# The mixture of 32 experts by sorted token rows instead of every expert on every token

## The reference, cut to what matters

```python
x2 = _layernorm(src, ln2_g, ln2_b)
sel = jax.nn.sigmoid(x2 @ sel_w)
scores, idx = jax.lax.top_k(sel, K)
gate = (jax.nn.one_hot(idx, E, dtype=sel.dtype) * scores[..., None]).sum(-2)
h = jax.nn.relu(jnp.einsum('bsd,edh->bseh', x2, keys))
moe_out = jnp.einsum('bseh,ehd,bse->bsd', h, values, gate)
return src + moe_out
```

## Time and profile before

| what | value |
|---|---|
| median of 3 runs | 2990.05 us (2985.18 to 2991.54) |
| the profiled execution: time, span | 2985.78 us, 2983.8 us |
| PE busy | 2806.0 us, 94% |
| POOL busy | 2039.4 us, 68% |
| DVE, ACT busy | 1951.9 us (65%), 1852.1 us (62%) |
| mean granted PE clock | 0.974 of full speed |

### The profile page before, as it was taken

One profiled execution on the slowest core, in us unless ns is written; L12 is line 12 of the kernel. 1 busy time (PEld: TensorE's weight loads), 2 busy tenths in 40 slices (PEclk: granted clock), 3 DMA queues, 4 the chain that ended last, 5 costly groups with the idle time before them and its releaser, 6 DMA issues. The chain is left out here.

```text
span 2983.8 us, 61682 instructions
## 1 busy us (share of the span) xinstructions
PE 2806.0 (94%) x20928; PEld 2255.4 (76%) x20928; DVE 1951.9 (65%) x4370; ACT 1852.1 (62%) x5109; POOL 2039.4 (68%) x2550
## 2 busy tenths in 40 slices
PE   7999797899799999998999989998999999899999
PEld 5888575688678888886888866665888888778887
DVE  5554586455378888886555467775888888755554
ACT  2332353333289999996444446777999999754444
POOL 4324663332278888875999975555888888689998
PEclk9999898999889999999999989999999999999999
DMA  3000563000122222223555565542222222255554
GB/s 110 6 1 3 131 139 86 1 1 1 31 44 44 55 54 44 44 58 128 186 185 188 197 165 110 108 98 47 47 60 47 44 44 44 68 198 204 191 190 167
DMA packets 152506, 266.05 MB, mean 89 GB/s; under 512 B 14099, under 2 KB 124947, under 8 KB 129139
## 3 DMA queue, kind: packets, MB, share of 16 engines
q1 hardware_dynamic: 152194, 262.11, 31.4%
HBM read 204.06 MB, written 53.67 MB: 86 GB/s over the span
## 5 line engine op out<-in xcount | busy, mean ns | idle before, releaser
L3150 POOL TENSOR_TENSOR f4m_ht_lo<-f4m_ht,f4m_ht_hi 128x512 fp32r<-128x512 f32 x256 | 330.6, 1310 | 36.8 <-ACT f4m_ht_hi L3075 23.8
L3150 POOL TENSOR_TENSOR f6m_ht_lo<-f6m_ht,f6m_ht_hi 128x512 fp32r<-128x512 f32 x256 | 331.2, 1310 | 31.3 <-ACT f6m_ht_hi L3075 17.0
L3120 DVE SCALAR_TENSOR_TENSOR f6m_ht<-f6m_hr,f6m_gate 128x512 f32<-128x512 f32 x256 | 176.3, 691 | 166.1 <-PE f6m_hr L2997 100.9
L3075 ACT ACTIVATE f4m_ht_hi<-f4m_ht 128x512 fp32r<-128x512 f32 x256 | 161.6, 632 | 192.7 <-DVE f4m_ht L3120 191.4
L3120 DVE SCALAR_TENSOR_TENSOR f4m_ht<-f4m_hr,f4m_gate 128x512 f32<-128x512 f32 x256 | 175.9, 690 | 160.9 <-PE f4m_hr L2997 94.9
L3075 ACT ACTIVATE f6m_ht_hi<-f6m_ht 128x512 fp32r<-128x512 f32 x256 | 161.7, 632 | 189.1 <-DVE f6m_ht L3120 188.9
L2671 ACT ACTIVATE f4a_pr<-f4a_sr,f4a_nm 128x256 f32<-128x256 f32 x512 | 243.6, 496 | 23.6 <-DVE f4a_nm L2739 23.0
L2671 ACT ACTIVATE f6a_pr<-f6a_sr,f6a_nm 128x256 f32<-128x256 f32 x512 | 243.5, 496 | 21.0 <-DVE f6a_nm L2739 20.5
L2825 POOL TENSOR_TENSOR f4a_rr<-f4a_tmp 128x256 f32<-128x256 f32 x256 | 187.1, 731 | 91.8 <-DVE f4a_tmp L2747 89.7
L2825 POOL TENSOR_TENSOR f6a_rr<-f6a_tmp 128x256 f32<-128x256 f32 x256 | 187.1, 731 | 82.5 <-DVE f6a_tmp L2747 80.0
L2747 DVE TENSOR_TENSOR f4a_tmp<-f4a_ur,f4a_turn 128x512 f32<-128x512 f32 x256 | 175.2, 685 | 61.4 <-PE f4a_ur L2536 57.6
(11 more groups left out here) (588 smaller groups left out, 9342.2 us busy)
## 6 DMA issues: line engine op xcount, KB each, us to landing
f4m_gate<-f4o_gates SPq DMA_DIRECT2D x64, 1024.0 KB, 4.7
f6m_gate<-f6o_gates SPq DMA_DIRECT2D x64, 1024.0 KB, 4.7
r_scratch<-r_parts SPq DMA_DIRECT2D x32, 192.0 KB, 2.3
all_qs<-r_scratch SPq DMA_DIRECT2D x16, 384.0 KB, 4.8
all_ks<-r_scratch SPq DMA_DIRECT2D x16, 384.0 KB, 6.7
f4al_scratch<-f4a_parts SPq DMA_DIRECT2D x32, 192.0 KB, 2.2
all_qs<-f4al_scratch SPq DMA_DIRECT2D x16, 384.0 KB, 5.0
all_ks<-f4al_scratch SPq DMA_DIRECT2D x16, 384.0 KB, 6.7
```

Of the source, the lines that this page charges most:

```text
L3075: nc.scalar.activation(ht_hi[:, n % RB, :], ht[:, n % RB, :], ACT.Copy).then_inc(hi_ready, 1)
L3120: nc.vector.scalar_tensor_tensor(ht[:, n % RB, :], hr[:, n % HB, :], 0.0, gate[:, q % GB, n % LOADED, :], ALU.max, ALU.mult).then_inc(ht_r ...
L3150: nc.gpsimd.tensor_tensor(ht_lo[:, n % RB, :], ht[:, n % RB, :], ht_hi[:, n % RB, :], ALU.subtract)\
```

## The change

The mixture no longer runs each expert on each token. Per half of the batches (a "sort", 2048 tokens, 8192 token-expert pairs):

1. In the attention, `Opening` finds for each token the four expert numbers, counts by a triangular matmul how many earlier tokens chose the same expert, and so gets four slot rows for each token (`gate_index` to `place_row`). POOL sends each 128-token tile to its slots in DRAM by four indirect transfers (`send`), eight for a batch, one after each of the steps 8 to 15. A region of 69632 rows for each sort leaves 2048 rows for each expert.
2. A short chain (`sort_counts` to `sort_table`) makes a table with the first row and the expert of each of 96 tiles of 128 slots.
3. The mixture block runs 48 rounds of four tiles. In a round SP loads four row numbers from the table to registers, issues four loads and, five rounds later, four stores to the same rows. PE loads four expert offsets to registers, then runs four transposes, four fp32 matmuls with keys, four transposes, four fp32 matmuls with values. Each of these quartets is of another round (r, r-1, r-2, r-3). ACT and DVE each empty two PSUM banks in a round.
4. When all stores of a sort have landed, POOL fetches the four results of each token tile by four indirect transfers (`fetch`), 64 for a sort. DVE adds them to x with the gate as a scalar (`mix`, eight operations for a batch). The first sort's fetches are issued while the second sort's rounds run, the second sort's after them.
5. The slots must be defined: in f1 and f3, SP writes 68 transfers of 512 KB of zeros over one region each.
6. The Forerun's instructions stand after the rounds instead of inside them; POOL's part of it stands ahead of the second sort's fetches.

```diff
+            region = w.slots[w.cleared * REGION:(w.cleared + 1) * REGION, :].rearrange("(n p r) c -> n p (r c)", p=P, r=FILL)
+            sp.wait_ge(zero_set, 1)
+            for n in range(REGION // (P * FILL)):
+                sp.dma_start(region[n], zero[:, :]).then_inc(zero_in, 16)
...
+    def gate_index(self, dve, i):
+        dve.wait_ge(self.gate_step, i * self.STEPS + 3)
         self.nc.vector.memset(self.spare[:, 1:2], 0.0)
         for t in range(TT):
-            last = self.nc.vector.match_replace(self.left[:, t, :], self.best[:, t, :], self.sel[:, t, :], 0.0)
+            last = self.nc.vector.max_index(self.index[:, t, :], self.best[:, t, :], self.sel[:, t, :])
         last.then_inc(self.gate_step, 1)
...
+    def send(self, pool, i, n):
+        if n == 0:
+            pool.wait_ge(self.row_ready, i + 1)
+            pool.wait_ge(self.x2_ready, (i + 1) * TT)
+        t, c = divmod(n, TOPK)
+        self.nc.gpsimd.indirect_dma_start(self.w.slots, bass.IndirectOffsetOnAxis(ap=self.row[:, i * TT + t, c:c + 1], axis=0),
+                                          self.x2[:, i % self.X2B, t, :], None).then_inc(self.sent[i % self.X2B], 16)
...
-                if n == 13 and it[0] == B + 1:
-                    opening.high_parts(pool)
+                if placed(it) is not None and n >= 8:
+                    opening.send(pool, placed(it), n - 8)
...
+                rows[r] = registers(sp, "row", r, 0)
+                if r >= XB:
+                    sp.wait_ge(x_turned, r - XB + 1)
+                for n in range(QUARTET):
+                    sp.dma_start(xr[:, r % XB, n, :], w.slots[bass.ds(rows[r][n], P), :]).then_inc(x_in[r % XB], 16)
+
+            def store(r):
+                sp.wait_ge(y_ready, r + 1)
+                for n in range(QUARTET):
+                    sp.dma_start(w.slots[bass.ds(rows[r][n], P), :], y[:, r % YB, n, :]).then_inc(y_out[r % YB], 16)
...
+            def hidden(r):
+                pe.wait_ge(xt_ready, r + 1)
+                if r:
+                    pe.wait_ge(h_ready, r)
+                for n in range(QUARTET):
+                    mm = nc.tensor.matmul(h_ps[:, n * P:(n + 1) * P], xt[:, r % 2, n * P:(n + 1) * P],
+                                          keys[:, bass.ds(experts[r][n], P)], start=True, stop=True)
+                mm.then_inc(h_made, 1)
...
+            for sort in range(SORTS):
+                for n in range(YB):
+                    pool.wait_ge(y_out[n], 16 * QUARTET * len(range(n, (sort + 1) * PER, YB)))
+                if sort and then is not None:
+                    for e in range(E1):
+                        then.gpsimd(pool, e)
+                for n in range(sort * NT // SORTS, (sort + 1) * NT // SORTS):
+                    fetch(n)
```

772 lines of the change are left out of this document (431 added, 341 removed).

## The result

The changed kernel takes 3050.48 us (median of four runs, 3049.89 to 3054.45), the kernel before 2990.8 in the same comparison: ratio 1.0212, 95% interval 1.0197 to 1.0227. It is 2.1% slower. The forecast was 2958 and faster; the time lies inside its range, on the wrong side of no change.

A forecast was written before the change was run, and what follows sets the result against it. PE and POOL were taken to bound the mixtures, with close busy shares in the attentions. Mixtures -132, sends +76, block ends +10 and DVE +14 gave -32, so 2958 us, range 2840 to 3110.

The forecast's parts named there:

- The mixtures: Both mixture blocks: f6m from 381 to 314 us, f4m from 383 to 318, together -132.
- the attention's sum: Both attentions: eight sends add 8.8 us to POOL's 27.25 a batch, a batch takes 2.7 us longer, +76 in all.
- The block's end: End of each attention: batch 13's sends end about 5 us after the old barrier, +10 for both.
- DVE in the attention: Some 14 small slot-row operations a batch more on DVE partly delay `tmp`: 0.5 us a batch, +14, bounds 0 and +60.
- PE's 3 to 5 small matmuls a batch fall in its new idle time: Attention: PE's added small matmuls were taken to fit its idle time, with no term in the sum.
- POOL's price c: POOL's own part of one indirect transfer, taken as 1.1 us; each 0.1 us of it is 37 us in all.
- POOL's price is higher: Rival for POOL's indirect transfers: at c = 1.5 the kernel takes 3104 us; decides from 1.19; chance 0.22.
- The register load: Mixture rounds: loading four row numbers to registers was taken as 0.6 us, bounds nothing and 1.8.
- SP's queue sets the round: Mixture rounds: SP's queue, not PE, sets a round of 4.7 us, bounds 3.9 and 6.1.
- PE's clock: Rival in the rounds: PE falls to 1.2 GHz and becomes the bound, +103, 3061 us; chance 0.10.
- DVE holds POOL's sends: Rival in the attention: DVE operations make a send cost 0.35 us more, +78, 3036 us; chance 0.08.
- Zeros: Stages f1 and f3: writing 35.7 MB in each takes 160 us but is covered, costing nothing.

The follow-up runs named there:

- e3: Changed kernel with the same sends spread, one after every second step instead of after each of steps 8 to 15: 2967.9 us.
- e7: Changed kernel with the eight sends of batch 13 moved from the attention to the mixture block: 3146.0 us.
- e1: Changed kernel without the indirect sends of batches 0 to 13, DVE and PE work for slot rows kept: 2901.6 us.
- e2: Changed kernel with every send kept but most of DVE's slot-row work left out, slot numbers a fixed pattern: 3022.9 us.
- e5: Kernel of e1 with PE's counting matmuls moved from step 1 to 0 and DVE's place from step 2 to 0: 2997.0 us.
- f3: Changed kernel with a round's four loads issued by ACT's queue, SP issuing only the stores: 3109.8 us, against 3176.9 for its control.
- e8: Changed kernel with every send moving 64 rows instead of 128, as many sends as before: 3210.3 us.

## Why the prediction was wrong

The mixtures came out as forecast and the attentions did not: +100 us were forecast for both attentions with their ends, and 205 were measured, 145 in the periods (90 forecast) and 60 at the ends (10).

**The step that failed** is the attention's sum: "27.25 + 8.8 = 36.05, over the 33.35 of now. POOL becomes the bound and a batch takes 2.7 us longer." It adds POOL's work over a batch, as if the free time of the steps without sends could pay for those with them. But all eight sends stand in steps 8 to 15, and the kernel lets POOL run no more than five heads ahead of PE (PE issues the products that POOL's sums start from five steps ahead). By step it is 0.74 + 0.745 + 1.15 = 2.64 us in eight steps and 2.08 in eight others, 37.8 us; measured 38.15. POOL was to be near 100% and is at 88% in the middle of the stage. With the sends spread evenly (e3) the batch takes 36.2, about the forecast's sum. That moved 59 us in the periods and 24 at the ends, 83 of the 105 missed, and turns the sign: 2967.9 against 2986.3 for the kernel before.

**The block's end**, "+10 for both", was +30 each. 16 of these go when batch 13's eight sends leave the attention (e7): some 6 because they end after DVE's last operation (1461.9 against 1456.0), which is the 5 of the forecast, and 10 for POOL's pause after its last send, for which no row of before stands. 9 more stand in e1 too (77.9 against 68.5), without any send in the attention, so they come with the slot rows and the mixture's start. The remaining 5 are not taken apart; the last iterations are slower by the sends as all others are.

**DVE in the attention**, 0.5 us a batch: 0.8 with sends (e2), 1.1 without (e1). Without sends it is not by making `tmp` late but by PE's waits at the desk bank, of which an earlier `place` takes 0.4 away (e5). With sends PE's waits there are 0.5 us a batch for `place` and 0.4 for `yn` in the changed kernel, and no run tells how much of the 0.8 they make. The prediction's sentence "PE's 3 to 5 small matmuls a batch fall in its new idle time" overlooked that they need a bank which something has to empty.

**POOL's price c** was 1.1 and is 1.15 in the attention and 1.26 for bare fetches, of which 64 took 81 us against 70. By the prediction's own prices (22.4 us for each 0.1 on the sends, 12.8 on the bare fetches) that is 11 + 20 = 31 us, which alone takes the forecast's -32 to nothing. So the size of c used up the gain, on paper, and the rival "POOL's price is higher", which decides from 1.19, had a part of the truth; the 60 us of loss came through the bunched sends and the end of the block, which were among no rivals.

**The mixtures**: 313 and 315 against 318 and 314 forecast, -136 against -132. Rounds take 4.5 us (4.7 forecast), and SP's eight issues 3.73 (3.84). The register load was priced high: SP's own took 0.30 us (median), under the 0.6 that the prediction took and the floor that it cites for it, so the measurement decides; with its four register operations and the gap it is 0.5, where 0.84 was taken. That SP's queue sets the round is shown by f3. That the sum came so close is in part luck: the shorter rounds (-7 each) stand against the longer fetches (+11).

**PE's clock** in the rounds was 0.83 to 1.00 of full speed in windows of 20 us, and PE waited 81 us for `f4m_xr` in the first mixture (21 of them ahead of the first round, most of that the block's end): loads and not PE set the pace, so that rival did not decide. **DVE holds POOL's sends**: a send is 0.98 us in the attention, beside a busy DVE, and 0.95 to 0.96 at its end, where DVE has nothing more to do, so it fell; where a hold shows, POOL holds DVE (e8). **Zeros**: they cost nothing, as forecast; f1, f3 and retention kept their times.

**What stays open**: why SP, ACT, DVE and with them PE nearly stop beside POOL's indirect transfers in three groups of experiments and hardly in the two others and the first run, with no difference in the kernel before. No chip served two groups of experiments. That it is the chip, and not the time or what else ran beside it, is theory G's reading, and it is not shown. Open too is what happens in the 10 us at a block's end, and why the attention f6a is about 1.4 us a batch longer than f4a in nearly every kernel, before too. A kernel in which direct and indirect transfers never overlap was not tried.

## What to carry to other kernels

When work is added to an engine inside a software pipeline, sum it by step and not by iteration, and ask how many steps ahead that engine may run: bunched, with the same sends in all, it cost 83 us here, more than the whole loss of 60. For everything that is added, list the buffer it passes through (the desk bank) and what the block's end waits for. At these sizes indirect transfers cost POOL per instruction (0.8 of 0.98 us), so the number of them decides. Whatever runs beside them, on any engine, should be measured on more than one chip.
